# Attention beside a ternary feed-forward: another order of the opening, bias rows in one partition, w1's ternary form in halves

## The reference

```python
x = L0_attn_x
xn = _layernorm(x, axis=-1)
# attention: z = layernorm(xn) * g + b; q, v = z @ w_q.T + b_q, z @ w_v.T + b_v; k = q
# scores = q k / 4; attn = softmax(scores); out = (attn v) @ w_out.T + b_out
# feed-forward: h = gelu(xn @ ternary(W1).T + b1); out = h @ ternary(W2).T + b2
# ternary(w): scale = max(mean |w|, 1e-8); clip(round(w / scale), -1, 1)
x = x + _L0_attn_ref(xn, ...) + _L0_ffn_ref(xn, ...)
```

## Time and profile before

| | |
|---|---|
| Time, median of 3 runs | 1397.49 us (1397.26 to 1397.63) |
| The profiled execution | 1398.74 us, its span 1397.0 us, mean granted clock 0.994 |
| Busy, share of the span | PE 1367.5 us (98%), DVE 1328.5 (95%), ACT 1236.8 (89%), POOL 141.4 (10%) |
| Chain that ended last, by line | DVE part_max L889 68%; PE L389 6%; PE L403, L1198, L359, L1115 3% each; DMA rows<-in_rows 1% |
| First of 40 slices (35 us) | PE 6, DVE 6, ACT 5, PEclk 8 tenths; DMA 239 GB/s |
| Loads of the opening | w1 and w2 issued at 1.65 and 1.63 us, the bias rows at 2.13; DMA share near 1.0 from 4 to 20 us, 0.08 from 22 to 24 |
| Where the span goes | groups to about 200 us, heads to the end |

### The profile page before, as it was taken

How to read it: one execution, slowest core, us unless ns; L and a number is a source line. 1 busy time by engine, 2 the same in 40 slices (tenths; PEclk the granted TensorE clock), 3 DMA queues, 4 the chain that set the end, 5 groups by cost and what they waited for, 6 DMA issues and landing times.

```text
span 1397.0 us, 32162 instructions
## 1 busy us (share of the span) xinstructions
PE 1367.5 (98%) x13350; PEld 467.5 (33%) x13350; DVE 1328.5 (95%) x1396; ACT 1236.8 (89%) x2244; POOL 141.4 (10%) x351
## 2 busy tenths in 40 slices
PE   6999999999999999999999999999999999999999
PEld 4656643222222222222222222222222222222244
DVE  6898999999999999999999999999999999999935
ACT  5564638999999999999999999899999999999975
POOL 2101034000000000000000000000222200002200
PEclk8999999999999999999999999999999999999999
DMA  6112000011110001001001001001122201012122
GB/s 239 27 38 65 31 18 2 33 32 33 33 33 33 32 33 33 33 33 33 33 33 33 32 31 35 26 28 39 51 64 60 63 32 34 33 35 63 40 89 98
DMA packets 33916, 61.75 MB, mean 44 GB/s; under 512 B 11392, under 2 KB 16928, under 8 KB 33514
## 3 DMA queue, kind: packets, MB, share of 16 engines
q1 hardware_dynamic: 33194, 58.04, 12.5%
q10 hardware_dynamic: 576, 1.65, 0.3%
HBM read 41.29 MB, written 16.77 MB: 42 GB/s over the span
## 4 chain that ended last, share of the span: by engine, by line
DVE 70%; PE 25%; issue 2%; DMA 1%; ACT 1%; POOL 0%; ACTq 0%; SPq 0%; DVEq 0%; POOLq 0%
DVE part_max L889 68%; PE ps L389 6%; PE ps L403 3%; PE ps L1198 3%; PE ps L359 3%; PE ps L1115 3%; PE ps L1135 2%; PE ps L480 2%; PE ps L461 1%; DMA rows<-in_rows 1%; ACT w L1092 1%; PE ps L450 1%; PE ps L490 0%; PE ps L1170 0%; DMA max_rows<-max_split 0%
## 5 line engine op out<-in xcount | busy, mean ns | idle before, releaser
L1092 ACT ACTIVATE w<-ps 128x512 f32<-128x512 f32 x2048 | 1109.5, 596 | 65.9 <-PE ps L403 16.5
L889 DVE TENSOR_REDUCE part_max<-ps 128x1 f32<-128x1024 f32 x1024 | 1161.1, 1212 | 4.1 <-PE ps L359 3.8
L389 PE MATMUL ps<-w,v_ones 128*32 128x256 f32 (+1 forms) x7688 | 627.8, 398 | 0.6 <-DVE resid L810 0.3
L403 PE MATMUL ps<-qry,key 50*128 50x512 f16 x1984 | 399.0, 387 | 7.7 <-ACT w L1092 6.9
L359 PE MATMUL ps<-qry,key 48*128 48x512 f16 x2048 | 393.9, 381 | 5.3 <-DVE part_max L889 5.3
L389 PEld LDWEIGHTS ps<-w,v_ones 128*32 128x32 f32 x7688 | 151.5, 108 | 313.2 <-issue 160.7
L403 PEld LDWEIGHTS ps<-qry,key 50*128 50x128 f16 x1984 | 98.1, 92 | 430.2 <-ACT w L1092 412.1
L359 PEld LDWEIGHTS ps<-qry,key 48*128 48x128 f16 x2048 | 99.9, 93 | 82.6 <-DVE part_max L889 16.6
L681 POOL COPY v_ones<-v_all 128x128 f32<-128x128 f32 x64 | 18.7, 293 | 748.8 <-PE ps L389 748.8
L1059 ACT ACTIVATE q_split<-q_by_factor,sigma_bq 128x512 f16<-128x512 f32 x16 | 11.1, 719 | 63.0 <-DVE q_by_factor L791 62.6
L1198 PE MATMUL ps<-x,w_ternary 128*128 128x512 f16 x256 | 62.4, 382 | 1.6 <-ACT hidden L1063 1.6
(11 more groups left out here) (151 smaller groups left out, 481.1 us busy)
## 6 DMA issues: line engine op xcount, KB each, us to landing
key<-q_parts SPq DMA_DIRECT2D x62, 128.0 KB
qry<-q_parts SPq DMA_DIRECT2D x62, 128.0 KB
o_heads<-o_evacuated SPq DMA_DIRECT2D x31, 256.0 KB, 9.8
key<-q_parts SPq DMA_DIRECT2D x66, 64.0 KB
qry<-q_parts SPq DMA_DIRECT2D x66, 64.0 KB
resid<-in_x SPq DMA_DIRECT2D x8, 512.0 KB, 13.7
q_parts<-q_split SPq DMA_DIRECT2D x16, 256.0 KB, 2.3
out<-resid SPq DMA_DIRECT2D x7, 512.0 KB, 4.7
```

What stands on the lines that cost most here:

```text
L389: mm = eng.matmul(pv[32 * c:32 * c + 2 * D, c0:c1], vst[:, kb, :], prob[kb % 2][:, c * BANK + c0:c * BANK + c1], start=(kb == 0), stop=(kb ...
L403: eng.matmul(ring_bank(v, i, False), key[v][r:r + KROWS, kb * P:(kb + 1) * P], qry[v][r:r + KROWS, c * BANK:(c + 1) * BANK], start=True, s ...
L889: dve.tensor_reduce(part_max[h % 2][:, blk, side:side + 1], pa[a % 2], AX.X, ALU.max).then_inc(s_r, 1)
L1092: act.activation(prob[kb % 2][:, c * BANK:(c + 1) * BANK], ring_bank(k, i, last), ACT.Exp, scale=exp_scale).then_inc(s_e, 1)
```

## The change

The bias rows come into one partition by a load of 4 KB, as the second of ScalarE's queue. Three products with a row of ones spread them over the partitions in PSUM: bq and bv in one bank, bo + b2 summed in another. ScalarE takes the magnitudes from there and copies bv and the sum; POOL's addition goes. On SyncE's queue the load of w2 waits until w1 has landed. TensorE does b1's sum and the two bound products first and signals; the products of b with wv and wq come behind and have a signal of their own. The magnitudes of w2 are summed on ScalarE ahead of wv's scaling. w1 is made ternary in two halves of the hidden units, one ahead of group 0's q, one behind it. `q_split` is cut in two functions (`q_factors`, `q_split`). w2's threshold and comparison stand before the norm of group 1, its difference behind. `out_scale` moves into group 1, wo's parts into group 2. Six more products of ones stand before the first q products.

```diff
-        row = sb("rows", [P, 4, C])
-        bq_row, bv_row, bo_row, b2_row = (row[:, n, :] for n in range(4))
+        row = sb("rows", [1, 4 * C])
+        bv_row = sb("bv_row", [P, C])
...
-        bound_o = tr_x[1][:, 0:C]
-        b_wq, sum_b1 = pq[1][:, C:C + KC], pq[1][:, C + KC:C + KC + 1]
+        bound_o = bank(3)[:, 0:C]
+        bq_rep, bv_rep, bias_rep = bank(3)[:, 0:C], bank(3)[:, C:2 * C], pf[1][:, 0:C]
+        b_wq, sum_b1 = pq[1][:, C:C + KC], tr_f[:, 0:1]
...
             sp.dma_start(wqv[:, :, :, :].rearrange("p i k c -> p (i k c)"), w_qv).then_inc(s_wqv, 16)
+            sp.wait_ge(s_w[0], 16)
             sp.dma_start(w2[:, :], w_2).then_inc(s_w[1], 16)
...
-            pool.wait_ge(s_row, 16)
-            pool.tensor_tensor(bias_row[:, :], bo_row, b2_row, ALU.add).then_inc(s_row, 1)
...
+            def ternary(j, src, dst, scratch, n):
+                dve.tensor_scalar(scratch, src, nhalf[:, j:j + 1], None, ALU.is_lt).then_inc(s_wd, 1)
+                dve.wait_ge(s_wd, n + 1)
+                dve.scalar_tensor_tensor(out=dst, in0=src, scalar=half[:, j:j + 1], in1=scratch, op0=ALU.is_gt,
                                          op1=ALU.subtract).then_inc(s_wd, 1)
+
+            def ternary_w1(i):
+                n0, n1 = i * FF // 2, (i + 1) * FF // 2
+                ternary(0, w1[:, :].rearrange("p (k n) -> p k n", k=KC)[:, :, n0:n1], w1t[:, :, n0:n1],
+                        below.rearrange("p (k n) -> p k n", k=KC)[:, :, n0:n1], 2 + 2 * i)
+
+            def below_w2():
+                threshold(1, 6)
+                dve.tensor_scalar(below, w2[:, :], nhalf[:, 1:2], None, ALU.is_lt).then_inc(s_wd, 1)
+
+            def ternary_w2():
+                dve.wait_ge(s_wd, 9)
+                dve.scalar_tensor_tensor(out=w2t[:, :, :].rearrange("p k n -> p (k n)"), in0=w2[:, :], scalar=half[:, 1:2],
+                                         in1=below, op0=ALU.is_gt, op1=ALU.subtract).then_inc(s_wd, 1)
...
+                dve.wait_ge(s_qb, 2)
+                dve.wait_ge(s_rb, 1)
                 dve.tensor_tensor(bqe_col[:, :], b_wq, bq_col, ALU.add)
-                dve.tensor_tensor(bv_sum[:, :], b_wv, bv_row, ALU.add)
+                dve.tensor_tensor(bv_sum[:, :], b_wv, bv_row[:, :], ALU.add)
...
-            ternary(0, w1, w1t)
-            stats_of(1)
+            threshold(0, 0)
+            ternary_w1(0)
+            q_factors(0)
             dve.wait_ge(s_wvs, KC + 1)
             dve.tensor_tensor(wvp[:, 1, :, :], wvs, wvp[:, 0, :, :], ALU.subtract).then_inc(s_wvp, 1)
+            ternary_w1(1)
+            stats_of(1)
             q_split(0)
+            below_w2()
             norm(1)
-            ternary(1, w2, w2t)
-            out_scale()
+            ternary_w2()
             results(0)
...
                 if g == 1:
+                    out_scale()
+                if g == 2:
                     dve.wait_ge(s_ow, KC + 1)
                     dve.tensor_tensor(wop[:, 1, :, :], wos, wop[:, 0, :, :], ALU.subtract).then_inc(s_op, 1)
...
+            act.dma_start(col[:, :], cols).then_inc(s_col, 16)
+            act.dma_start(row[:, :], rows).then_inc(s_row, 16)
             act.dma_start(idf[:, :], ident).then_inc(s_id, 16)
-            act.dma_start(col[:, :], cols).then_inc(s_col, 16)
             act.dma_start(w1[:, :], w_1).then_inc(s_w[0], 16)
-            act.dma_start(row[:, :, :].rearrange("p n c -> p (n c)"), rows.to_broadcast((P, 4 * C))).then_inc(s_row, 16)
...
-            act.wait_ge(s_row, 16)
-            act.activation(bv_abs[:, :], bv_row, ACT.Abs)
-            act.activation(bq_abs[:, :], bq_row, ACT.Abs).then_inc(s_abs, 1)
+            act.wait_ge(s_rp, 1)
+            act.activation(bv_abs[:, :], bv_rep, ACT.Abs)
+            act.activation(bq_abs[:, :], bq_rep, ACT.Abs).then_inc(s_abs, 1)
+            act.activation(bv_row[:, :], bv_rep, ACT.Copy).then_inc(s_rb, 1)
+            act.wait_ge(s_rp, 2)
+            act.activation(bias_row[:, :], bias_rep, ACT.Copy).then_inc(s_rb, 1)
             abs_sum(0, w1)
...
                     scaled(wq, gq_col, wqs, wqp, s_wqs)
+                    abs_sum(1, w2)
                     scaled(wv, gv_col, wvs, wvp, s_wvs)
                     factor_rows(g)
-                    abs_sum(1, w2)
...
                 if first:
                     abs_total(0)
+                    pe.wait_ge(s_sg, 4)
                 factor_transposes(g)
                 if first:
+                    pe.wait_ge(s_rb, 2)
+                    for n in range(KEEP):
+                        pe.matmul(pf[1][:, 0:P], ones[:, :], ones[:, :], start=True, stop=True)
                     pe.wait_ge(s_wqp, 1)
...
                 for f in range(KF):
+                    if first and f == KF // 2:
+                        pe.wait_ge(s_wd, 6)
...
+            pe.wait_ge(s_row, 16)
+            pe.matmul(bank(3), ones[0:1, :], row[:, 0:2 * C], start=True, stop=True).then_inc(s_rp, 1)
+            pe.matmul(bias_rep, ones[0:1, :], row[:, 2 * C:3 * C], start=True, stop=False)
+            pe.matmul(bias_rep, ones[0:1, :], row[:, 3 * C:4 * C], start=False, stop=True).then_inc(s_rp, 1)
...
+            def row_products(out, reps, w):
+                for k in range(KC):
+                    mm = pe.matmul(out, reps[:, k, :], w[:, k, :], start=(k == 0), stop=(k == KC - 1))
+                return mm
+
+            pe.wait_ge(s_abs, 1)
+            pe.matmul(sum_b1, ones[:, :], b1abs[:, KF:KF + 1], start=True, stop=True)
             pe.wait_ge(s_abs, 2)
             pe.wait_ge(s_sg, 2)
...
+            row_products(bound_q, reach_rep, absq)
+            row_products(bound_v, reach_rep, absv).then_inc(s_qb, 1)
+            row_products(b_wv, b_rep, wv)
...
-            pe.matmul(sum_b1, ones[:, :], b1abs[:, KF:KF + 1], start=True, stop=True).then_inc(s_qb, 1)
+            mm.then_inc(s_qb, 1)
```

More of the change, by code:

```diff
@@ L36 @@
 WARM = 16
+KEEP = 6
 PERIOD = "BBAPBBAPBBAPBBAP"
@@ L240, in attention_ffn @@
         s_row = sem("rows_loaded")
+        s_rp = sem("rows_replicated")
+        s_rb = sem("bias_rows_copied")
         s_wqv = sem("wq_wv_loaded")
@@ L701, in _ @@
             split_max(0)
-            pool.wait_ge(s_row, 17)
+            pool.wait_ge(s_rb, 2)
             for g in range(NG):
@@ L729, in _, with threshold @@
             dve.memset(ones[:, :], 1.0).then_inc(s_c, 1)
-            def ternary(j, src, dst):
-                n = 4 * j
+            def threshold(j, n):
                 dve.wait_ge(s_wp, j + 1)
@@ L741, in ternary @@
                 dve.wait_ge(s_wd, n + 2)
-                dve.tensor_scalar(below, src[:, :], nhalf[:, j:j + 1], None, ALU.is_lt).then_inc(s_wd, 1)
-                dve.wait_ge(s_wd, n + 3)
-                dve.scalar_tensor_tensor(out=dst[:, :, :].rearrange("p k n -> p (k n)"), in0=src[:, :],
-                                         scalar=half[:, j:j + 1], in1=below, op0=ALU.is_gt,
+            def ternary(j, src, dst, scratch, n):
+                dve.tensor_scalar(scratch, src, nhalf[:, j:j + 1], None, ALU.is_lt).then_inc(s_wd, 1)
+                dve.wait_ge(s_wd, n + 1)
+                dve.scalar_tensor_tensor(out=dst, in0=src, scalar=half[:, j:j + 1], in1=scratch, op0=ALU.is_gt,
                                          op1=ALU.subtract).then_inc(s_wd, 1)
+            def ternary_w1(i):
[9 more added lines that the diff above has]
+                                         in1=below, op0=ALU.is_gt, op1=ALU.subtract).then_inc(s_wd, 1)
             def stats_of(g):
@@ L791, in q_split @@
                     dve.tensor_tensor(qt[:, k, :], pq[k], f_row[:, :], ALU.mult).then_inc(s_qf, 1)
+            def q_split(g):
                 wait(dve, s_qs, 16 * KC * g)
@@ L878, in results @@
                     if g == 0 and i == 0:
-                        dve.wait_ge(s_wd, 8)
+                        dve.wait_ge(s_wd, 10)
                     part = [p[:, 2 * i:2 * i + 2, :] for p in parts_of(g)]
@@ L922, in _ @@
                     add_ffn(g - 1, j)
+                q_factors(g)
                 q_split(g)
@@ L1048, in group @@
                     factor_rows(g)
-                    if g == 1:
+                    if g == 2:
                         act.wait_ge(s_od, 5)
@@ L1064, in group @@
                     if f % 2:
-                        if first and f == 1:
-                            act.wait_ge(s_wd, 4)
+                        if first and f in (1, 3):
+                            act.wait_ge(s_wd, 4 if f == 1 else 6)
                         act.wait_ge(s_g, KF * g + f + 1)
@@ L1164, in group @@
                 if g == 1:
-                    pe.wait_ge(s_wd, 5)
+                    pe.wait_ge(s_wd, 7)
+                if g == HALF_GROUPS:
                     pe.wait_ge(s_od, 1)
@@ L1215, in _ @@
                 pe.matmul(pf[1][:, 0:P], ones[:, :], ones[:, :], start=True, stop=True)
+            pe.wait_ge(s_row, 16)
[8 more added lines that the diff above has]
```

(11 more changed lines are left out.)

2 lines of the change are left out of this document (1 added, 1 removed).

## The result

The change makes the kernel a little slower: **1400.98 us**, median of 10 runs (1398.42 to 1402.2), against 1397.71 of before on the same chip (10 runs, 1397.04 to 1398.73). The ratio is 1.002, 95% interval 1.0012 to 1.0028. The medians are 3.3 us apart. That is outside the predicted range and a little over the 2.8 us that the prediction took as what a measurement can tell from no change. The profiled execution took 1401.13 us, its span 1399.3, at a mean granted clock of 0.994. (The granted clock is the share of full speed that the profile gives for TensorE: 1.00 is its upper level, 0.50 its lower.)

What follows compares the result with a forecast made beforehand. Opening bound by the bias-row load, then TensorE's pace, then from about 215 us VectorE's row maxima; opening savings reach the end one to one. Sum: -4.5 -1.2 +5.5 +0.1 = -0.1 us, median 1397.4, range 1394.9 to 1399.4.

Steps and rivals of the forecast that it cites:

- 1, bias rows: Opening: a 4 KB row load lands at 6.2 to 6.9 us, and VectorE's bounds start at 10.95 instead of 15.44.
- 4.5 us earlier: Start of VectorE's bounds in the opening, 10.95 instead of 15.44 us; entered the sum as -4.5 us.
- the two bound products, four again: TensorE in the opening: the bound products take the 1.97 us of four earlier products and end at 10.9.
- step 3: Clock before group 0's q: nearly 5 us idle brings the lower level, q products take 5.07 us, ending at 25.0.
- 2, magnitudes of w2: ScalarE, ahead of wv: 1.9 us is given back, so the q products start 2.6 us earlier, not 4.5.
- 4, VectorE's order: VectorE newly waits for q, 3.6 and 1.9 us, +5.5 in the sum; first hidden fix-up at 37.06 instead of 37.31.
- 5, output scale: Its 1.21 us leave the stretch before the first hidden fix-up (-1.2) and cost +0.1 where it now stands.
- 6, loads: Opening loads: w1 lands at 8.7 us (bounds 8.1 to 11.7), w2 from 13.3 to 17.3; taken as costing nothing.
- A: Rival: the clock holds or returns at once, q products end at 22.5; -2.6 us, 1394.9 us; chance 0.14.
- B: Rival: VectorE never waits for q and keeps the 4.5 and 1.21 us; -5.6 us, 1391.9 us; chance 0.05.
- C: Rival: w2's load lands late, at 22.2 us, and ScalarE waits for it; +6.3 us, 1403.8 us; chance 0.08.
- D: Rival: the bias row load is no faster, lands at 13.6, bounds at 18; +6.9 us, 1404.4 us; chance 0.02.

Runs made afterwards that it cites:

- e1: The changed kernel with the bias rows in a zero-filled tile of 128 partitions and spreading products using all 128: 1397.82 us, ratio to before 1.0.
- e3: The changed kernel with w2's magnitudes summed behind the factor rows again, as before the change: 1398.41 us, ratio to before 0.9999.
- c1: The changed kernel with full rows in the spreading products, w2's magnitudes behind the factor rows and 14 extra products instead of 6: 1394.65 us, ratio to before 0.9974.
- c2: The changed kernel, one-row products kept, with w2's magnitudes behind the factor rows and 14 extra products instead of 6: 1396.34 us, ratio to before 0.9983.
- e6: The changed kernel with full rows in the spreading products and w2's magnitudes behind the factor rows, 6 extra products kept: 1395.97 us, ratio to before 0.9987.
- c3: c1 with the output scale and wo's parts back where the kernel before has them: 1396.08 us, ratio to before 0.9986.
- e5: e1 without SyncE's wait for w1, so w2's load is issued at once: 1398.34 us, ratio to before 1.0003.
- e2: The changed kernel with 22 instead of 6 extra products of ones ahead of group 0's q products: 1397.33 us, ratio to before 0.9998.
- c4: c1 with 22 extra products of ones instead of 14: 1395.39 us, ratio to before 0.9979.

## Why the prediction was wrong

It gave 1397.4 us and a range to 1399.4; measured is 1400.98.

**1, bias rows: the step that failed.** Row load, spreading and order came out as said. The term "4.5 us earlier" was 2.42, since the step "the two bound products, four again" took 1.97 us from the earlier trace rows, a row at the upper level, and they ran in 3.48 at the lower. Of the 2.07 lost, 1.51 are this. The other 0.56 come from the warming products, which end 0.74 later than the 6.6 taken from before, as their records come closer later in that execution. With the 0.5 that the steps behind it missed, this makes the fix-up 39.61 instead of 37.06. At q after loses another 0.8 against e1, 4.99 us against 4.15, since the clock, low at q's start in both, comes back later; whether the first fall causes that is not shown. In step 3 I asked only whether TensorE is idle; what also matters is how many partitions its products use. e1 gives the forecast's opening and its time. The time agrees partly by luck: e1's fix-up, 36.37, is 0.7 earlier than the forecast's, since its q products took 4.15 us and not the 5.07 of the sum.

The premise that what the opening saves reaches the end one to one held within about one us: from the opening of group 2 to the end of the span it is 1336.9 us before, 1336.7 after, and 1335.7 to 1338.2 in all the versions.

**2, magnitudes of w2: right.** From bounds to factor rows 8.55 us, predicted 8.2 (10.95 to about 19.2); e3 gives the 1.9 back (e1's factor rows start 2.2 later, its bounds 0.3).

**3, clock in the q products: right.** 4.60 us of idle, the lower level, 4.99 us; six extra products don't bridge it. Fourteen do in c1 and c2, where the factor rows come 1.9 us sooner behind the bounds; with them so soon, six were enough in e6 and not in e3.

**4, VectorE's order: right.** Waits 3.66 and 1.52, predicted 3.6 and 1.9. A half of w1 takes 0.75 + 1.28 us, 0.2 more than the half of the whole; from wv's part behind the second q (27.93) to the fix-up it is 11.68, predicted 11.31.

**5, output scale:** right in kind, -0.76 for -1.1 (c3).

**6, loads: right.** w1 lands at 9.8, inside the bounds of 8.1 and 11.7 but 1.1 later than taken; w2 takes 4.7. In the kernel after ScalarE waits for neither. The Trainium skill (DMA: Bandwidth & Descriptors, "Rules for kernel authors") speaks for issuing w2 early. The runs show neither gain nor loss from it: e5, which does so, is within 0.3 us of e1 at the fix-up. The 4.4 us that the prediction estimated for w2 by the same page's fit, which the page measured on loads issued by GpSimd, are near the 4.7 of this load on SyncE's queue.

**Rivals.** A (clock holds at q) is what e2 and c1 make by design. c1 comes nearest to B: VectorE still waits 1.03 us for q, and the time is 1394.65, not 1391.9. C and D did not occur. The slower side came through a mechanism that I had not listed, and I had counted "an unbroken start from 1 to 15" in favour of the clock.

**The range** assumed that the opening varies no more than before. Before, the bound products end at 10.54 and ScalarE waits for the load of the bias rows until 14.6, so their pace can't show; with the load gone it does. The ten times lie 3.8 us apart, against 1.7 before. That this is the reason is argued: c3 and c4, with full rows, spread nearly as wide, and e6 does not.

## What to carry over

When a wait for a load is removed, look at what was hidden in it: here TensorE's clock in the opening. Give small products that stand between a warm start and work on the critical path all partitions (zeros did here), and price such work at both levels of the clock. Fill an idle stretch with products up to, not past, the event that ends it (22 instead of 14 moved the fix-up 1.15 us later); and put a sum that nobody awaits yet behind the row that TensorE awaits.
